# GpSimd waits for the spread of the scores of rounds 2 to 4

## The chip, the cores and the metric

The kernel runs on one core of one Trainium2 chip. The metric is the time of one execution on the device, in microseconds; several executions are taken and the median is given. The engines of the core are named as in the profile: PE is TensorE (matmuls), DVE is VectorE, ACT is ScalarE, POOL is GpSimd, SP is SyncE. They run side by side, each through its own list of instructions in order, and wait for each other by semaphores.

## The reference

The input `x` holds 128 sequences of 32 tokens with 128 features. A first block makes a gated recurrent layer with a normalization at its end, a second one a feed-forward layer for half of the tokens of each sequence.

```python
# first block (cut)
ctx = causal_ema(x, tau_ctx)
wg = sigmoid(einsum(concat[x, ctx], Wg) + bg);  gated = x * wg
mod = 0.5 + sigmoid(einsum(gelu(x @ Wn1.T + bn1), Wn2) + bn2)     # 128 time constants
traces = causal_ema(gated * mod, tau) for each of them
temporal = sum over them of traces * softmax(blend)
gate = sigmoid(temporal @ Wtemp.T + btemp);  soma = gelu(x @ Wsoma.T + bsoma)
out = (soma * gate) @ Wout.T
hidden = (out - mean) / sqrt(var + 1e-05) * gamma + beta
# second block (cut)
scores = einsum('bsd,d->bs', hidden, w_router)
top_scores, top_idx = top_k(scores, 16)                            # 16 of 32 tokens
h = gelu(selected @ W1 + b1);  processed = h @ W2 + b2
result = x + hidden, and at the selected tokens + sigmoid(top_scores) * processed
```

## The kernel before

The 4096 tokens are worked on in five rounds, of 1, 2, 2, 2 and 1 quads; a quad is 512 tokens, or four tiles of 128. The kernel is software-pipelined by hand: the string `ORDER` lists all steps as `kind:round.part`, and each engine walks through this one list and issues what it has to do of each step. So every engine executes its part in the order of `ORDER`, and steps of different rounds are interleaved in it. PE writes its results to a ring of eight PSUM banks, which other engines read.

The steps of a round, as far as they matter here:

- `unit` (16 for each round): PE multiplies (L1042), DVE multiplies the result by the gated input into one of three buffers `prod` (L817), POOL adds that to `ctx_acc` (L468). `sum` is POOL's last addition of a round (L476). `gate`: PE multiplies `ctx_acc` (L1049), ACT takes the tanh (L612). `soma_gate` is DVE's product of the two (L826, into `x_t`).
- `out`: PE (L1057), then ACT squares and copies to `o_sb` (L619, L631); `stats`: DVE adds the squares (L835); `var`: POOL adds the epsilon (L480) and takes the power -0.5 (L483).
- `score`: DVE multiplies the router's column of `o_sb` by that power, 8 numbers on each partition, 4 in rounds 0 and 4 (L842, into `small`), and lays the scores on a diagonal mask (L846, into `spread`), which raises `spread_done` by one.
- `bc`: PE multiplies `spread` by a matrix of ones within a sequence (L1061); DVE compares (L855, L856) and counts with `tie` (L863, L866). `pick`: DVE makes the selection matrix (L875, into `pick`) and weights it (L883, into `pick_w`, from `small` and `pick`).
- `normed`: ACT scales `o_sb` (L636, L639). `gather` (PE L1070, ACT L652, DVE L902), `up` (PE L1093 and L1098, ACT's gelu L673), `turn_pick` (PE L1081, ACT L663), `down` (PE L1109, DVE L907) and `scatter` (PE L1117, DVE L916 into `x_nat`) are the feed-forward layer. DMAs of SP then write `x_nat` out.
- `plus_beta` (POOL, L457: `x_nat` + beta) and `residual` (POOL, L491 and L496: `o_sb` times gamma, then added to `x_nat`) make the residual, which DVE's `scatter` of the same round needs.

In the late part of `ORDER` the steps around the three scores stand like this (steps of `unit` and `back` that stand between are cut where a line has "..."):

```
sum:3 unit:4.2 stats:2.1 var:2 carry:4.0 gather:1 unit:4.9 unit:4.8 gate:3 up:1.0 up:1.1 soma_gate:3
score:2 residual:1 scatter:0 normed:2 unit:4.5 out:3.0 unit:4.11 bc:2 tie:2 turn_pick:1 pick:2 down:1 ...
sum:4 stats:3.1 var:3 score:3 up:2.0 up:2.1 scatter:1 gate:4 bc:3 tie:3 soma_gate:4 normed:3 turn_pick:2
plus_beta:2 pick:3 down:2 plus_beta:3 residual:2 out:4.0 gather:3 stats:4.0 var:4 scatter:2 turn_pick:3
up:3.0 up:3.1 score:4 bc:4 normed:4 tie:4 pick:4 down:3 plus_beta:4 residual:3 gather:4 scatter:3 up:4.0 ...
```

POOL has nothing to do for `score`: it goes from `var:3` to `plus_beta:2`, for instance, as soon as PE has read `x_nat` for the last time.

Of the kernel before, what the change touches and what calls it, by code (L numbers as in the profile page):

```python
# [44 lines left out]
def tiles(r):  # L45
    return QUADS[r] * QT
# [138 lines left out]
def adaln_ffn(nc, x, tau_raws, w_n2, b_n2, blend, tau_ctx, w_g, b_g, w_n1, b_n1, w_soma, b_soma,  # L185
              w_temp, b_temp, w_out, gamma, beta, w_router, w_1, b_1, w_2, b_2, out):
    with ExitStack() as ctx:
# [204 lines left out]
        @block.gpsimd  # L392
        def _(pool):
            nc.gpsimd.memset(ident[:, :], 0.0).then_inc(own_pool, 1)
            pool.wait_ge(own_pool, 1)
            nc.gpsimd.affine_select(out=ident[:, :], in_=ident[:, :], compare_op=ALU.not_equal, fill=1.0,
                                    base=0, pattern=[[-1, P]], channel_multiplier=1).then_inc(ident_done, 1)
            nc.gpsimd.memset(ones[:, :], 1.0).then_inc(ident_done, 1)
            nc.gpsimd.memset(odd_even[:, :], 1.0).then_inc(own_pool, 1)
            nc.gpsimd.memset(eye_t[:, :], 0.0).then_inc(own_pool, 1)  # L400
            nc.gpsimd.memset(before[:, :], 1.0).then_inc(own_pool, 1)
            nc.gpsimd.memset(same_b[:, :, :], 1.0).then_inc(own_pool, 1)
            nc.gpsimd.memset(minus_half[:, :], -0.5).then_inc(own_pool, 1)
            nc.gpsimd.iota(rank_of[:, :], pattern=[[1, T], [0, BT]], base=0, channel_multiplier=0,
                           allow_small_or_imprecise_dtypes=True).then_inc(own_pool, 1)
            pool.wait_ge(own_pool, 7)
            for b in range(BT):
                rows = slice(b * T, (b + 1) * T)

                nc.gpsimd.affine_select(out=odd_even[rows, 0:1], in_=odd_even[rows, 0:1], compare_op=ALU.is_ge,  # L410
                                        fill=0.0, base=L - 1, pattern=[[0, 1]],
                                        channel_multiplier=-1).then_inc(masks_done, 1)
                nc.gpsimd.affine_select(out=odd_even[rows, 1:2], in_=odd_even[rows, 1:2], compare_op=ALU.is_ge,
                                        fill=0.0, base=-L, pattern=[[0, 1]],
                                        channel_multiplier=1).then_inc(masks_done, 1)
                nc.gpsimd.affine_select(out=eye_t[rows, :], in_=eye_t[rows, :], compare_op=ALU.not_equal, fill=1.0,
                                        base=0, pattern=[[-1, T]], channel_multiplier=1).then_inc(masks_done, 1)
                nc.gpsimd.affine_select(out=before[rows, :], in_=before[rows, :], compare_op=ALU.is_ge, fill=0.0,
                                        base=-1, pattern=[[-1, T]], channel_multiplier=1).then_inc(masks_done, 1)
            pool.wait_ge(masks_done, 4 * BT)  # L420
            places = rank_of[:, :].rearrange("p (j b) -> p b j", b=BT)
            for src, fill in ((places, -1.0), (same_b[:, :, :], 0.0)):
                nc.gpsimd.affine_select(out=src, in_=src, compare_op=ALU.is_ge, fill=fill, base=0,
                                        pattern=[[-T, BT], [0, T]], channel_multiplier=1).then_inc(own_pool, 1)
            pool.wait_ge(own_pool, 9)
            for src, fill in ((places, -1.0), (same_b[:, :, :], 0.0)):
                nc.gpsimd.affine_select(out=src, in_=src, compare_op=ALU.is_ge, fill=fill, base=T - 1,
                                        pattern=[[T, BT], [0, T]], channel_multiplier=-1).then_inc(masks_done, 1)
            owned = [9]

            def pool_owned():
                owned[0] += 1
                return owned[0]

            for step in STEPS:
                kind, r, k = step
                if kind == "table":
                    pool.wait_ge(powers_done, 1)
                    pool.wait_ge(turned_c, 1)
                    lags = slice(k * TG, (k + 1) * TG)  # L440
                    nc.gpsimd.tensor_tensor(decayed[:, lags, :], blend_w[:, None, :].to_broadcast([P, TG, E]),
                                            powers[:, lags, None].to_broadcast([P, TG, E]),
                                            ALU.mult).then_inc(full_tab, 1)
                elif kind == "powers":
                    pool.wait_ge(powers_done, 1)
                    for t in range(L):
                        last = nc.gpsimd.tensor_copy(falling[:, :, t:t + 1],
                                                     powers[:, None, L - 1 - t:L - t].to_broadcast([P, HT, 1]))
                    last.then_inc(falling_done, 1)
                elif kind == "plus_beta":  # L450
                    pool.wait_ge(full(("xt", r, 0)), filled(("xt", r, 0)))
                    if r not in SCANNED:
                        pool.wait_ge(full(("context", r, 0)), filled(("context", r, 0)))
                    if r == 0:
                        pool.wait_ge(rest_in, 2 * 16)
                    x_r = tiles_of(x_nat, r)
                    nc.gpsimd.tensor_tensor(x_r, x_r, beta_r[:, None, :].to_broadcast([P, tiles(r), E]),  # L457
                                            ALU.add).then_inc(xb_done, 1)
                elif kind == "unit" and k > 0:
                    n = PRODS.index(step)  # L460
                    dst = lagged(part(ctx_acc, r), r, k, shift=1)
                    pool.wait_ge(read(step), reads_after(step))
                    if add_before(step):
                        pool.wait_ge(acc_done, ADDED[add_before(step)])
                    else:
                        first = ("unit", r, 0)
                        pool.wait_ge(read(first), reads_after(first))
                    nc.gpsimd.tensor_tensor(dst, dst, packed(prod[:, n % NP, 0:width(r)], r, k),  # L468
                                            ALU.add).then_inc(acc_done, 1)
                elif kind == "sum":  # L470
                    for h in range(QUADS[r]):
                        back = ("back", r, h)
                        pool.wait_ge(read(back), reads_after(back))
                    pool.wait_ge(acc_done, ADDED[add_before(step)])
                    dst = part(ctx_acc, r)[:, L * batches(r):]
                    nc.gpsimd.tensor_tensor(dst, dst, carried[:, r % 2, 0:L * batches(r)],  # L476
                                            ALU.add).then_inc(acc_done, 1)
                elif kind == "var":
                    pool.wait_ge(stats_done, nth(last_of("stats", r)))
                    nc.gpsimd.tensor_scalar(small[:, r % 2, 4, 0:tiles(r)], small[:, r % 2, 5, 0:tiles(r)], 1e-5, None,  # L480
                                            ALU.add).then_inc(own_pool, 1)
                    pool.wait_ge(own_pool, pool_owned())
                    nc.gpsimd.tensor_tensor(small[:, r % 2, 7, 0:tiles(r)], small[:, r % 2, 4, 0:tiles(r)],  # L483
                                            minus_half[:, 0:tiles(r)], ALU.pow).then_inc(rstd_done, 1)
                elif kind == "residual":
                    pool.wait_ge(norm_done, BEFORE[r + 1] * QT)
                    if r:
                        pool.wait_ge(res_done, r)
                    else:
                        pool.wait_ge(scanned, len(SCANS))  # L490
                    nc.gpsimd.tensor_tensor(prod_res[:, 0:tiles(r), :], o_sb[:, r % 2, 0:tiles(r), 0:E],  # L491
                                            gamma_r[:, None, :].to_broadcast([P, tiles(r), E]),
                                            ALU.mult).then_inc(own_pool, 1)
                    pool.wait_ge(own_pool, pool_owned())
                    pool.wait_ge(xb_done, r + 1)
                    nc.gpsimd.tensor_tensor(tiles_of(x_nat, r), tiles_of(x_nat, r), prod_res[:, 0:tiles(r), :],  # L496
                                            ALU.add).then_inc(res_done, 1)
# [650 lines left out]
```

## Time and profile before

| | us |
|---|---|
| median of 3 runs | 192.11 |
| lowest and highest | 189.43, 192.43 |
| the profiled execution | 189.27 |
| its span, first to last instruction | 187.5 |

In the span PE is busy for 92%, DVE for 77%, POOL for 72% and ACT for 51%. The chain of work that ended last lies on PE for 76% of the span, on DVE for 11% and on POOL for 3%; among its lines on DVE are L842 and L846, with 3% of the span each. The table of costliest groups has POOL's L468 with 81.0 us in 75 instructions. The busy times are modelled for matmuls, so a PE that is 92% busy is not a PE at its peak. A share of the whole span says little about one stretch; the rows below are therefore taken from the timeline, where "[3.72 <-DVE spread L846]" behind an instruction means that its engine stood idle for 3.72 us before it, until DVE's L846 let it go.

### The profile page before, as it was taken

The page shows a single profiled execution, that of the slowest core. Times are in us where ns is not written, and L with a number is a line of the kernel's source. Part 1 is how long each engine was busy: PE and PEld are TensorE (multiplying, and loading weights), DVE is VectorE, ACT ScalarE, POOL GpSimd, SP SyncE. Part 2 cuts the span into 40 slices and gives each one's busy share as a digit, 9 for nine tenths or more (in the row PEclk, how much of TensorE's full clock was granted, in tenths as well). Part 3 has the DMA queues.
Part 4 walks back from the last instruction along what each step waited for, and adds up shares of the span by engine and source line. Part 5 has one row for each costly group of instructions (what it writes and reads, how often), then busy time and mean ns, then how long its engine had stood idle before and what let it go on. Part 6 is the DMA issues. An engine that isn't in the chain of part 4 may idle for free.

```text
span 187.5 us, 3480 instructions
## 1 busy us (share of the span) xinstructions
PE 172.6 (92%) x1154; PEld 130.4 (70%) x1154; DVE 143.6 (77%) x223; ACT 96.5 (51%) x177; POOL 134.8 (72%) x158
## 2 busy tenths in 40 slices
PE   5798999999999999999999999999999983994991
PEld 4485445877669588695769687688689943983881
DVE  1628897769997988859787887798789749858822
ACT  3548697264680141772505454578487465157030
POOL 7838000788897999979686988999797599529800
PEclk9999999999999999999999999999999997899999
DMA  5687000000000000000000000000002000303032
GB/s 128 167 209 201 0 3 0 0 2 5 0 0 0 3 0 3 0 0 0 3 2 0 0 3 2 0 0 3 2 0 59 0 2 0 112 3 112 0 112 59
DMA packets 12785, 5.62 MB, mean 30 GB/s; under 512 B 2880, under 2 KB 12640, under 8 KB 12768
## 3 DMA queue, kind: packets, MB, share of 16 engines
q1 hardware_dynamic: 11904, 5.20, 10.3%
q10 hardware_dynamic: 864, 0.20, 0.5%
q8 instruction: 10, 0.16, 0.4%
q14 instruction: 7, 0.06, 0.1%
HBM read 3.30 MB, written 2.10 MB: 29 GB/s over the span
## 4 chain that ended last, share of the span: by engine, by line
PE 76%; DVE 11%; issue 3%; POOL 3%; ACT 2%; DMA 2%; ACTq 0%; DVEq 0%; POOLq 0%
PE ring L1042 27%; PE ring L1109 6%; PE ring L1015 5%; PE ring L1026 4%; PE ring L999 4%; PE ring L978 4%; PE ring L1000 4%; PE ring L1049 4%; DVE small L842 3%; PE ring L1057 3%; DVE spread L846 3%; PE ring L1006 2%; PE ring L1032 2%; PE ring L992 2%; PE ring L966 2%
## 5 line engine op out<-in xcount | busy, mean ns | idle before, releaser
L468 POOL TENSOR_TENSOR ctx_acc<-ctx_acc,prod 128x256 f32<-128x256 f32 (+17 forms) x75 | 81.0, 1095 | 30.9 <-DVE prod L817 26.8
L817 DVE TENSOR_TENSOR prod<-ring,gm 128x256 f32<-128x256 f32 (+17 forms) x75 | 41.3, 577 | 8.9 <-PE ring L1042 7.4
L1042 PE MATMUL ring<-mod_hi,decayed_lo 128*128 128x512 f32 (+15 forms) x104 | 35.0, 374 | 0.0
L1042 PE MATMUL ring<-mod_lo,decayed_hi 128*128 128x512 f32 (+15 forms) x104 | 30.1, 326 | 0.0
L1042 PE MATMUL ring<-mod_hi,decayed_hi 128*128 128x512 f32 (+15 forms) x104 | 30.0, 327 | 0.0
L1042 PEld LDWEIGHTS ring<-mod_hi,decayed_lo 128*128 128x128 f32 x104 | 18.4, 189 | 7.6 <-issue 6.3
L1042 PEld LDWEIGHTS ring<-mod_lo,decayed_hi 128*128 128x128 f32 x104 | 19.2, 189 | 2.0 <-issue 1.2
L1042 PEld LDWEIGHTS ring<-mod_hi,decayed_hi 128*128 128x128 f32 x104 | 19.2, 189 | 0.9
L804 DVE TENSOR_TENSOR state<-ring,blend_w 128x1024 f32<-128x1024 f32 x16 | 18.8, 1219 | 1.1 <-PE ring L1015 0.9
L1109 PE MATMUL ring<-w_sb,gm 128*128 128x128 f32 x128 | 15.8, 282 | 0.1
L1109 PEld LDWEIGHTS ring<-w_sb,gm 128*128 128x128 f32 x128 | 15.4, 199 | 0.3 <-issue 0.3
L673 ACT ACTIVATE gm<-ring,b_c 128x512 f32<-128x512 f32 (+1 forms) x20 | 10.8, 599 | 4.8 <-PE ring L1098 4.5
L602 ACT ACTIVATE carried_nat<-ring 128x512 f32<-128x512 f32 x8 | 4.8, 598 | 15.2 <-PE ring L1026 15.2
L496 POOL TENSOR_TENSOR x_nat<-x_nat,prod_res 128x1024 f32<-128x1024 f32 (+1 forms) x5 | 10.0, 2008 | 0.4
L639 ACT ACTIVATE o_sb<-o_sb,small 128x128 f32<-128x128 f32 x32 | 9.8, 392 | 0.0
L457 POOL TENSOR_TENSOR x_nat<-x_nat,beta_r 128x1024 f32<-128x1024 f32 (+1 forms) x5 | 9.6, 1927 | 0.3 <-DMA gamma_r<-in_L_cond_gamma_dram 0.3
L612 ACT ACTIVATE ring<-ring,bias_h 128x1024 f32<-128x1024 f32 (+1 forms) x5 | 4.6, 918 | 9.6 <-PE ring L1049 9.6
L772 DVE TENSOR_TENSOR_SCAN ring<-prod_res,ring 128x1024 f32<-128x1024 f32 (+1 forms) x4 | 8.0, 2017 | 1.9 <-ACT x_t L532 1.7
L999 PE MATMUL ring<-x_t,turned_w 128*128 128x512 f32 x16 | 8.8, 634 | 0.5 <-ACT ctx_acc L532 0.5
L1061 PE MATMUL ring<-spread,same_b 128*128 128x256 f32 (+1 forms) x10 | 3.3, 412 | 6.5 <-DVE spread L846 6.5
L491 POOL TENSOR_TENSOR prod_res<-o_sb,gamma_r 128x1024 f32<-128x1024 f32 (+1 forms) x5 | 9.1, 1820 | 0.1
L1015 PE MATMUL ring<-gated_nat,mod_nat 32*128 32x256 f32 x128 | 9.2, 400 | 0.0
(168 smaller groups left out, 358.9 us busy)
## 6 DMA issues: line engine op xcount, KB each, us to landing
x_nat<-in_x_dram SPq DMA_DIRECT2D x3, 512.0 KB, 4.2
out_dram<-x_nat SPq DMA_DIRECT2D x3, 512.0 KB, 3.2
x_nat<-in_x_dram SPq DMA_DIRECT2D x2, 256.0 KB, 4.7
w_sb<-in_L_ffn_W_dram SPq DMA_DIRECT2D x2, 256.0 KB, 5.3
out_dram<-x_nat SPq DMA_DIRECT2D x2, 256.0 KB, 3.2
down<-in_cond_dram SPq DMA_DIRECT2D x2, 64.0 KB, 2.7
prod<-in_L_cond_Wg_dram ACTq DMA_DIRECT2D x1, 128.0 KB, 2.8
prod<-in_L_cond_Wsoma_dram ACTq DMA_DIRECT2D x1, 64.0 KB, 2.9
```

The source lines that it names most:

```text
L457: nc.gpsimd.tensor_tensor(x_r, x_r, beta_r[:, None, :].to_broadcast([P, tiles(r), E]), ALU.add).then_inc(xb_done, 1)
L468: nc.gpsimd.tensor_tensor(dst, dst, packed(prod[:, n % NP, 0:width(r)], r, k), ALU.add).then_inc(acc_done, 1)
L491: nc.gpsimd.tensor_tensor(prod_res[:, 0:tiles(r), :], o_sb[:, r % 2, 0:tiles(r), 0:E], gamma_r[:, None, :].to_broadcast([P, tiles(r), E]), ...
L496: nc.gpsimd.tensor_tensor(tiles_of(x_nat, r), tiles_of(x_nat, r), prod_res[:, 0:tiles(r), :], ALU.add).then_inc(res_done, 1)
L639: nc.scalar.activation(o_sb[:, r % 2, n, 0:E], o_sb[:, r % 2, n, 0:E], ACT.Copy, scale=small[:, r % 2, 7, n:n + 1]).then_inc(norm_done, 1)
L673: nc.scalar.activation(inner(r, f * n_sel, (f + 1) * n_sel), slot(step)[:, i * BANK:i * BANK + n_sel], ACT.Gelu_apprx_tanh, bias=b1_c[:, f ...
L804: nc.vector.tensor_tensor(state[:, q % 2, half, :], slot(step).rearrange("p (n e) -> p n e", e=E)[:, half, :], blend_w[:, None, :].to_broa ...
L817: nc.vector.tensor_tensor(dst, packed(slot(step), r, k), lagged(gated(r), r, k), ALU.mult).then_inc(read(step), 1)
L999: nc.tensor.matmul(dst[:, half], wgx_t, part(x_t, r)[:, half], start=True, stop=False)
L1015: last = nc.tensor.matmul(dst[:, at:at + 2 * E], mod_nat[rows, q % 2, i, :], gated_nat[rows, q % 2, i, :, :].rearrange("p o e -> p (o e)") ...
L1042: last = nc.tensor.matmul(to[:, c], w[:, k, :], src[:, c], start=(i == 0), stop=(i == len(parts) - 1))
L1109: last = nc.tensor.matmul(dst[:, n * E:(n + 1) * E], inner(r, at, at + P), w2_sb[:, f, :], start=first, stop=final)
```

## The change

In POOL's walk through `ORDER` a branch is added: at `score` of rounds 2, 3 and 4 POOL waits until DVE has written the spread of this round. POOL's next instruction is then L491 of `residual:1` in round 2, L457 of `plus_beta:2` in round 3 and L457 of `plus_beta:4` in round 4. No instruction is added, taken away or moved on any engine. Rounds 0 and 1 stay as they are.

```diff
@@ -482,6 +482,9 @@
                     pool.wait_ge(own_pool, pool_owned())
                     nc.gpsimd.tensor_tensor(small[:, r % 2, 7, 0:tiles(r)], small[:, r % 2, 4, 0:tiles(r)],
                                             minus_half[:, 0:tiles(r)], ALU.pow).then_inc(rstd_done, 1)
+                elif kind == "score" and r >= 2:
+
+                    pool.wait_ge(spread_done, r + 1)
                 elif kind == "residual":
                     pool.wait_ge(norm_done, BEFORE[r + 1] * QT)
                     if r:
```

## Rows read from the trace of the kernel before

**Rows 1.** The page, part 1: busy time, share of the span, instructions.

```profile
PE 172.6 (92%) x1154; PEld 130.4 (70%) x1154; DVE 143.6 (77%) x223; ACT 96.5 (51%) x177; POOL 134.8 (72%) x158
```

**Rows 2.** Timeline of DVE: start us, us, line, operation, count, idle before.

```profile
90.63 0.16 DVE L842 TENSOR_TENSOR small<-o_sb,small 128x4 f32<-128x4 f32 x1
90.83 0.29 DVE L846 TENSOR_TENSOR spread<-eye_t,small 128x128 f32<-128x128 f32 x1
...
137.99 1.89 DVE L842 TENSOR_TENSOR small<-o_sb,small 128x8 f32<-128x8 f32 x1
...
152.59 2.30 DVE L842 TENSOR_TENSOR small<-o_sb,small 128x8 f32<-128x8 f32 x1 [2.85 <-POOL small L483]
154.92 2.53 DVE L846 TENSOR_TENSOR spread<-eye_t,small 128x256 f32<-128x256 f32 x1
157.37 1.21 DVE L916 TENSOR_TENSOR x_nat<-ring,x_nat 128x1024 f32<-128x1024 f32 x1
158.82 0.43 DVE L855 TENSOR_TENSOR ring<-ring,small 128x256 f32<-128x256 f32 x1 [0.24 <-PE ring L1061]
...
162.78 0.69 DVE L883 SCALAR_TENSOR_TENSOR pick_w<-small,pick 128x512 f32<-128x512 f32 x1
...
169.03 1.25 DVE L842 TENSOR_TENSOR small<-o_sb,small 128x4 f32<-128x4 f32 x1 [0.34 <-POOL small L483]
170.32 2.23 DVE L846 TENSOR_TENSOR spread<-eye_t,small 128x128 f32<-128x128 f32 x1
173.19 0.30 DVE L855 TENSOR_TENSOR ring<-ring,small 128x128 f32<-128x128 f32 x1 [0.64 <-PE ring L1061]
...
175.34 1.09 DVE L883 SCALAR_TENSOR_TENSOR pick_w<-small,pick 128x256 f32<-128x256 f32 x1
176.76 0.69 DVE L907 TENSOR_TENSOR down<-ring,b_r 128x512 f32<-128x512 f32 x1 [0.33 <-PE ring L1109]
```

**Rows 3.** Timeline of POOL, same columns.

```profile
137.66 2.19 POOL L491 TENSOR_TENSOR prod_res<-o_sb,gamma_r 128x1024 f32<-128x1024 f32 x1
...
147.10 2.62 POOL L468 TENSOR_TENSOR ctx_acc<-ctx_acc,prod 128x192 f32<-128x192 f32 x4 [2.96 <-DVE prod L817]
...
150.88 1.67 POOL L483 TENSOR_TENSOR small<-small,minus_half 128x8 f32<-128x8 f32 x1
152.52 4.64 POOL L457 TENSOR_TENSOR x_nat<-x_nat,beta_r 128x1024 f32<-128x1024 f32 x2
157.12 2.37 POOL L491 TENSOR_TENSOR prod_res<-o_sb,gamma_r 128x1024 f32<-128x1024 f32 x1
...
167.65 0.23 POOL L480 TENSOR_SCALAR small<-small 128x4 f32<-128x4 f32 x1 [5.73 <-DVE small L835]
...
174.97 1.18 POOL L491 TENSOR_TENSOR prod_res<-o_sb,gamma_r 128x512 f32<-128x512 f32 x1
```

**Rows 4.** Timeline of PE, same columns.

```profile
141.59 3.74 PE L1109 MATMUL ring<-w_sb,gm 128*128 128x128 f32 x32
...
152.74 1.13 PE L1049 MATMUL ring<-ctx_acc,wtemp_t 128*128 128x512 f32 x2
157.59 1.19 PE L1061 MATMUL ring<-spread,same_b 128*128 128x256 f32 x2 [3.72 <-DVE spread L846]
...
159.43 4.30 PE L1109 MATMUL ring<-w_sb,gm 128*128 128x128 f32 x32
...
165.43 1.16 PE L1117 MATMUL ring<-down,pick_t 64*128 64x128 f32 x16
...
172.69 0.46 PE L1061 MATMUL ring<-spread,same_b 128*128 128x128 f32 x2 [2.75 <-DVE spread L846]
```

**Rows 5.** Windows of PE: stretch, us, busy, granted clock, DMA share, GB/s.

```profile
140.00:150.00 10.00, 10.00 (x84) 1.00 0.10 28
157.50:159.00 1.50, 1.41 (x4) 0.50 0.00 0
```

**Rows 6.** Timeline of ACT, same columns as rows 2.

```profile
168.61 2.63 ACT L673 ACTIVATE gm<-ring,b_c 128x512 f32<-128x512 f32 x4 [0.80 <-PE ring L1098]
```

## The prediction

> **What bounds the kernel now.** I read the page first: PE is busy for 92% of the span, POOL for 72%, DVE for 77% [rows 1]. A change to what POOL waits for can pay only where PE is not the limit, so I went down PE's own timeline and looked for its idle time. From 140 to 150 us it is busy throughout [rows 5]. Later it has two pauses: 3.72 us ahead of `bc:3` and 2.75 us ahead of `bc:4`, both ended by DVE's `spread` of L846 [rows 4]. `bc` stands ahead of the rest of PE's queue (`turn_pick`, `down`), so in both places everything waits for a score.
>
> The timeline of DVE says why the score is late [rows 2]. L842 multiplies 128x8 numbers. In round 0 its 128x4 form takes 0.16 us; in round 3 it takes 2.30 us, in round 4 1.25 us, in round 2 1.89 us. L846 takes 0.29 us in round 0 for 128x128, and 2.53 us (128x256) and 2.23 us (128x128) in rounds 3 and 4. The timeline of POOL [rows 3] shows what lies beside them: POOL ends its power (L483) at 152.55 and goes straight on to two L457 additions of 2.32 us each, from 152.52 to 157.16. L842 ends at 154.89, at the boundary between the two; L846 ends at 157.45, behind the second. So a DVE instruction of this kind that finds POOL busy stands until POOL's instruction ends. L883 in round 4 does so too: 1.09 us for 128x256, ending at 176.43, beside a POOL L491 from 174.97 to 176.15, though the 128x512 form in round 3 takes 0.69 us with POOL free. All three read both inputs from SBUF; L855 reads PSUM and SBUF and takes 0.43 us at 158.82, in the middle of a POOL multiplication [rows 2, 3].
>
> The Trainium skill, page "SBUF — State Buffer", the part on the engines' ports, says the same of a DVE instruction with two SBUF inputs against a GpSimd instruction that reads SBUF: exclusive, held for the whole instruction, and whichever starts first keeps it. It adds nothing to the sum, but by that rule a POOL that is made late can block a later DVE instruction as well as it blocked this one. The rows show this in L883 of round 4, and it is the main deduction below.
>
> **The change part by part.** It adds three waits, removes and moves nothing. Each holds POOL until the spread is written; what stands behind on POOL is `residual:1` in round 2, `plus_beta:2`, `plus_beta:3`, `residual:2`, `var:4` in round 3, `plus_beta:4`, `residual:3`, `residual:4` in round 4.
>
> Round 2. The two DVE instructions would run from 137.99 to about 138.6, where L842 alone lasted until 139.88; POOL, done with its additions at 137.66, resumes at 138.7, late by 1.0 us. It had 2.96 us of idle time at 147.10 [rows 3], so that is hidden; without that cover it costs 1.0 us. The gain of some 1.7 us on DVE meets a PE that has no gap here, so I take 0.1 us for it, with bounds of 0 and 0.3 (`down:1` on PE starts at 141.59 at any rate [rows 4]). I leave it out of the sum.
>
> Round 3. From the power's end at 152.55: L842 0.16 and L846 0.42 (twice the columns of the 0.29, 0.13 more) with 0.05 of dispatch each end at 153.2. POOL resumes at 153.3, 0.75 us late. PE is done with `gate:4` between 153.4 and 153.9 (1.13 us from 152.74 [rows 4]), so `bc:3` starts at 153.4 and not at 157.59. DVE's `scatter:1` (1.21 us) follows the spread and ends at 154.45; there L855 starts, which stood at 158.82: 4.4 us earlier. With the same steps between, L883 is ready at 162.78 - 4.4 = 158.4. POOL then is at: L457 153.3 to 155.6, L457 to 157.95, L491 (2.37) to 160.3. So L883 waits 1.9 us for L491 and ends at about 160.9. POOL's L496 (as many elements as L491, taken as 2.35) comes behind it and ends at 160.9 + 2.35 = 163.3.
>
> PE has meanwhile, at its full clock, done `bc`, `turn_pick` and `down:2` in 0.5 + 0.4 + 3.7 (the 3.74 at 141.59; at 159.43 it was 4.30), until 158.1, `out:4` and `gather:3` in about 0.9 each, until 159.9. It waits for DVE's `down:2`, which is behind L883: 160.9 + 0.69 = 161.6. So `scatter:2` starts at 161.6 and not at 165.43: 3.8 us earlier. The granted clock was 0.50 in 157.5 to 159.0, behind PE's long pause, that is 1.2 GHz [rows 5]; with the pause gone I expect 2.4 GHz there. That saves PE some 1.3 us, which is inside the wait for DVE and is no term.
>
> Round 4. DVE needs three instructions of 0.69 behind L883 up to `stats:4`: 162.9. POOL is free at 163.3; L480 and L483 took 1.35 us (167.65 to 169.00), so the power ends at 164.65 against 169.00. L842 and L846 end at 165.2. PE, from `scatter:2` at 161.6, has 4.5 us of work up to the end of `up:3` (165.43 to 169.94 before, where its idle 2.75 us began), so it is at `bc:4` at 166.1 against 172.69: 6.6 us earlier. `down:3` follows at 166.4; ACT's four activations of `up:3` (168.61, 2.63 us [rows 6]) move with `up:3` to 164.8 and end at 167.4, in time for its second half. It ends at 170.1.
> L883 is ready 2.15 us behind L855 (173.19 and 175.34), at 166.55 + 2.15 = 168.7. POOL: L457 165.25 to 166.5, L491 to 168.7, L496 2.35 more, to 171.1. This is a coin toss: L883 slips in between at 168.7 or waits until 171.1 and ends at 171.5. DVE's `down:3`, before at 176.76, then starts at 170.1 or at 171.5: 6.6 or 5.3 us earlier. What follows is a chain through DVE and PE with POOL soon done, and moves as a whole. **Sum: 5.3 to 6.6, I take 5.9 us.**
>
> The profiled execution took 189.27 us for a span of 187.5, so the sum gives 183.4. It lies by the lowest of the three runs (189.43); the other two are 2.7 and 3.0 higher and no row says why. From the median of 192.11 the sum is 186.2. Between the two I take 185.0.
>
> **The rivals.**
> (a) The stall moves to L883 nearly whole. For it speaks the 1.09 us at 175.34. POOL's next instruction could take hold ahead of DVE in round 3 too, so that L883 waits for L491 and L496, 2.35 us more. Then `scatter:2` is at 163.95, `bc:4` at 168.5, L883 of round 4 waits until 172.9, `down:3` starts at 173.3: a gain of 3.5 us, 185.8 from the profiled time and 188.6 from the median. Against it: L491 and L496 are parted by a wait of POOL for itself.
> (b) Nothing meets POOL later: L883 is free in both rounds. `scatter:2` starts at 159.9, PE reaches `bc:4` at 164.4, but POOL's power still ends at 164.0: a gain of 8.3 us, 181.0 or 183.8. Against it: POOL is busy without a pause from 153.3 to 162.7 by my times.
> (c) The wait does not bring it. If L842 and L846 were slow of themselves in the late rounds, the spread would come as late as before and POOL 4.9 us later: but POOL's `residual:2` has 5.73 us of idle behind it, so 0 to 1 us is lost, 189 to 193. The 0.16 and 0.29 of round 0 speak against it, and so do the ends that fall on POOL's ends.
> (d) Slower. In round 2 POOL waits for DVE, whose `score:2` stands behind `soma_gate:3`, which waits for ACT's tanh of `gate:3`. POOL's additions of round 4 (`unit:4.5` onward) lead to `sum:4`, `gate:4` and the third power, all on the path. It decides from a pause of 2.96 us on; by the rows it is 1.0. If the spread of round 2 came 6 us later than I have it, POOL would lose 4 us, offset by the gains of rounds 3 and 4 above. To end over 2% slower it would have to be 12 us later; or those gains fail as in (c), and the pause is 7 us: 195 to 196. Nothing in the rows points there.
>
> **How the numbers follow.** Forecast 0.60 (183.4 to 186.8 with the toss and the two bases), (a) 0.15, (b) 0.08, (c) 0.12, (d) 0.05. The range runs from 181.5, which keeps nearly all of (b), to 188.5, which keeps most of (a). Two per cent is 3.8 us (about what a measurement of this kernel can tell from no change). Forecast and (b) are faster by more, except where an unlucky spread between runs takes a part (0.03 of the forecast); a third of (a) is faster, the rest is within 2% with (c): faster 0.70, same 0.25, slower 0.05.
>
> **What would show it.** L842 and L846 in rounds 2 to 4 at 0.2 and 0.3 to 0.45 us each; POOL idle for about 1.0, 0.7 and 0.6 us, ended by `spread`; PE's gaps of 3.72 and 2.75 us ahead of `bc` gone, and the granted clock at its upper level near 158; L883 of round 3 at some 2.5 us, with a new gap of PE ahead of `scatter:2`. The forecast is wrong if L842 stays at 1 us or more, if L883 waits in neither round or for two of POOL's instructions, or if POOL's idle time at 147 is gone.

## The result and the profile after

| | before | changed |
|---|---|---|
| median, us (lowest to highest) | 191.91 (189.43 to 192.43) | 184.19 (184.11 to 185.21) |
| profiled execution, us | 189.27 | 184.11 |
| its span, us | 187.5 | 181.5 |

The changed kernel is faster: the ratio is 0.965, with a 95% interval of 0.955 to 0.975. Ratios, here and below, leave out executions over 1.5% above the fastest of the same kernel, while medians are taken over all, so the two differ a little (184.19 / 191.91 is 0.960). From here on line numbers of the changed kernel are three higher behind POOL's new branch: L845, L849 and L886 are the L842, L846 and L883 of before. The whole trace runs 0.5 us earlier than before already ahead of the first of the three waits (L845 of round 2 starts at 137.48, before at 137.99), so 5.5 of the 6.0 us of span belong to the change. The time of the profiled execution fell by only 5.2 us, because what lies outside the span grew from 1.8 to 2.6 us there; in the other three executions of the changed kernel it is 1.8 to 2.6.

The timeline of DVE in the changed kernel (start us, us, line, operation, count, idle before), beside [rows 2]:

```profile
137.48 0.16 DVE L845 TENSOR_TENSOR small<-o_sb,small 128x8 f32<-128x8 f32 x1
137.68 0.42 DVE L849 TENSOR_TENSOR spread<-eye_t,small 128x256 f32<-128x256 f32 x1
...
151.97 0.17 DVE L845 TENSOR_TENSOR small<-o_sb,small 128x8 f32<-128x8 f32 x1 [2.74 <-POOL small L483]
152.18 0.42 DVE L849 TENSOR_TENSOR spread<-eye_t,small 128x256 f32<-128x256 f32 x1
...
157.80 2.25 DVE L886 SCALAR_TENSOR_TENSOR pick_w<-small,pick 128x512 f32<-128x512 f32 x1
...
166.17 0.16 DVE L845 TENSOR_TENSOR small<-o_sb,small 128x4 f32<-128x4 f32 x1 [0.34 <-POOL small L483]
166.36 0.29 DVE L849 TENSOR_TENSOR spread<-eye_t,small 128x128 f32<-128x128 f32 x1
...
169.46 0.97 DVE L886 SCALAR_TENSOR_TENSOR pick_w<-small,pick 128x256 f32<-128x256 f32 x1
170.87 0.69 DVE L910 TENSOR_TENSOR down<-ring,b_r 128x512 f32<-128x512 f32 x1 [0.45 <-PE ring L1112]
```

The six instructions of the three scores take 0.16 to 0.42 us each; L842 and L846 had taken 2.30 and 2.53 us in round 3. L886 of round 3 takes 2.25 us, though; it had taken 0.69. `down:3` (L910) starts at 170.87 and not at 176.76.

The timeline of POOL in the changed kernel, beside [rows 3]:

```profile
138.18 2.20 POOL L494 TENSOR_TENSOR prod_res<-o_sb,gamma_r 128x1024 f32<-128x1024 f32 x1 [0.98 <-DVE spread L849]
...
146.49 2.61 POOL L468 TENSOR_TENSOR ctx_acc<-ctx_acc,prod 128x192 f32<-128x192 f32 x4 [2.12 <-DVE prod L820]
...
152.68 4.68 POOL L457 TENSOR_TENSOR x_nat<-x_nat,beta_r 128x1024 f32<-128x1024 f32 x2 [0.74 <-DVE spread L849]
157.31 2.19 POOL L494 TENSOR_TENSOR prod_res<-o_sb,gamma_r 128x1024 f32<-128x1024 f32 x1
159.58 2.67 POOL L499 TENSOR_TENSOR x_nat<-x_nat,prod_res 128x1024 f32<-128x1024 f32 x1
164.78 0.23 POOL L480 TENSOR_SCALAR small<-small 128x4 f32<-128x4 f32 x1 [2.53 <-DVE small L838]
...
166.73 1.27 POOL L457 TENSOR_TENSOR x_nat<-x_nat,beta_r 128x512 f32<-128x512 f32 x1 [0.60 <-DVE spread L849]
167.96 2.18 POOL L494 TENSOR_TENSOR prod_res<-o_sb,gamma_r 128x1024 f32<-128x1024 f32 x1
```

The three waits are the pauses of 0.98, 0.74 and 0.60 us ended by the spread, L849. The idle time ahead of the additions at 146.49 has shrunk from 2.96 to 2.12 us: the pause of round 2 was paid from it. L886 of round 3, which starts at 157.80, ends at 160.05, behind the L494 that ends at 159.50.

The timeline of PE in the changed kernel, same columns, beside [rows 4]:

```profile
153.21 0.59 PE L1064 MATMUL ring<-spread,same_b 128*128 128x256 f32 x2
...
154.08 3.74 PE L1112 MATMUL ring<-w_sb,gm 128*128 128x128 f32 x32
...
160.91 1.16 PE L1120 MATMUL ring<-down,pick_t 64*128 64x128 f32 x16 [1.32 <-DVE down L910]
...
163.52 0.47 PE L1096 MATMUL ring<-hid_hi,w_lo 128*128 128x512 f32 x1 [0.86 <-ACT hid_hi L655]
...
166.80 0.46 PE L1064 MATMUL ring<-spread,same_b 128*128 128x128 f32 x2 [0.28 <-DVE spread L849]
```

And that of ACT:

```profile
162.29 0.60 ACT L634 ACTIVATE o_sb<-ring 128x516 f32<-128x516 f32 x1 [2.94 <-POOL x_nat L499]
```

The pauses of 3.72 and 2.75 us ahead of `bc` are now nothing and 0.28 us. In their place stand 1.32 us ahead of `scatter:2`, which waits for DVE's `down:2` behind L886, and 0.86 us ahead of `up:3`, which waits for ACT's `hid_hi`. ACT's copy to `o_sb` (L634) stood for 2.94 us until POOL's L499 of `residual:2` was done: that wait is new.

The windows of PE in the changed kernel (stretch, us, busy, granted clock, DMA share, GB/s), beside [rows 5]:

```profile
156.00:160.00 4.00, 3.58 (x33) 1.00 0.15 41
```

The granted clock is 1.00, the level of 2.4 GHz, where it had been 0.50 between 157.5 and 159. `down:2` takes 3.74 us (L1112 at 154.08) and not 4.30.

### The profile page after: what moved, and what is told of

The parts are those of the page before. It is cut to its first block, busy times and chain, and to the rows that moved or that the text cites. A ratio compares the mean times of both kernels' runs of the same rounds, so it can differ in the third digit from the quotient of the medians.

```text
span 181.5 us, 3482 instructions
## 1 busy us (share of the span) xinstructions
PE 170.3 (94%) x1154; PEld 128.6 (71%) x1154; DVE 136.3 (75%) x223; ACT 96.3 (53%) x177; POOL 134.6 (74%) x158
## 4 chain that ended last, share of the span: by engine, by line
PE 76%; DVE 7%; POOL 7%; issue 4%; DMA 2%; ACT 1%; DVEq 0%; POOLq 0%; ACTq 0%
PE ring L1045 29%; PE ring L1018 5%; PE ring L1029 4%; PE ring L1112 4%; PE ring L981 4%; PE ring L1052 4%; PE ring L1060 3%; PE ring L1002 3%; DVE ring L775 2%; PE ring L1003 2%; PE ring L1096 2%; PE ring L1009 2%; DMA x_nat<-in_x_dram 2%; PE ring L1035 2%; PE ring L995 2%
## 5 line engine op out<-in xcount | busy, mean ns | idle before, releaser
L468 POOL TENSOR_TENSOR ctx_acc<-ctx_acc,prod 128x256 f32<-128x256 f32 (+17 forms) x75 | 81.0, 1098 | 29.8 <-DVE prod L820 25.7
L1112 PE MATMUL ring<-w_sb,gm 128*128 128x128 f32 x128 | 15.2, 276 | 0.1
L1112 PEld LDWEIGHTS ring<-w_sb,gm 128*128 128x128 f32 x128 | 14.7, 192 | 0.3 <-issue 0.3
L457 POOL TENSOR_TENSOR x_nat<-x_nat,beta_r 128x1024 f32<-128x1024 f32 (+1 forms) x5 | 9.6, 1927 | 1.3 <-DVE spread L849 1.3
L499 POOL TENSOR_TENSOR x_nat<-x_nat,prod_res 128x1024 f32<-128x1024 f32 (+1 forms) x5 | 10.1, 2016 | 0.4
L494 POOL TENSOR_TENSOR prod_res<-o_sb,gamma_r 128x1024 f32<-128x1024 f32 (+1 forms) x5 | 9.0, 1791 | 1.1 <-DVE spread L849 1.0
L1060 PE MATMUL ring<-wout_t,x_t 128*128 128x129 f32 x64 | 8.5, 276 | 0.0
```

The costliest lines, as they stand in the source:

```text
L1060: last = nc.tensor.matmul(dst[:, at:at + OW], part(x_t, r)[:, (k * QT + n) * P:(k * QT + n + 1) * P], wout_t[:, :], start=True, stop=True)
L1112: last = nc.tensor.matmul(dst[:, n * E:(n + 1) * E], inner(r, at, at + P), w2_sb[:, f, :], start=first, stop=final)
```

## The experiments

Ratios are against the kernel before, each with its 95% interval. The kernels were compared with before in several groups, so a difference between two of them is one between medians of different comparisons, good to some tenths of a microsecond.

| run | median, us | ratio |
|---|---|---|
| wait of round 2 alone | 191.36 | 1.004 (0.998 to 1.010) |
| wait of round 3 alone | 188.38 | 0.988 (0.979 to 0.996) |
| wait of round 4 alone | 186.93 | 0.981 (0.972 to 0.989) |
| changed kernel, `plus_beta:3` behind `residual:2` | 183.73 | 0.959 (0.953 to 0.965) |
| changed kernel, `plus_beta` early | 181.85 | 0.954 (0.944 to 0.964) |
| no waits, `plus_beta` early | 183.73 | 0.960 (0.953 to 0.966) |
| no waits, memset for `plus_beta:2` and `:3` | 188.46 | 0.983 (0.976 to 0.991) |
| changed kernel, also held until `pick_w` | 188.98 | 0.988 (0.981 to 0.995) |
| `plus_beta` early, waits, `residual:3` held | 181.08 | 0.948 (0.943 to 0.953) |

Where the interval reaches across 0.98 (the waits of round 3 and of round 4 alone, the memset), the kernel is faster, but whether by two per cent is not decided.

**The waits one by one.** The edit, for round 2 (3 and 4 likewise):

```diff
-                elif kind == "score" and r >= 2:
+                elif kind == "score" and r == 2:
```

> Only the wait of round 2 is kept. My theory (PE has no pause in round 2): the stall of L842 there goes (1.9 us to 0.2 us), POOL pauses for 1.0 us, its idle time ahead of the round 4 additions shrinks from 2.96 to about 2.1 us, and the time is that of before within 0.5 us. The stalls of rounds 3 and 4 stay: L842 and L846 together 4.8 and 3.5 us. Rival (every stall of DVE removed is time gained, or the change as a whole works through the earlier start): 1.7 us faster than before.

> Only the wait of round 3 is kept. My theory: bc of round 3 starts some 4 us earlier, then the chain waits for POOL's residual:2 as in the changed kernel, and round 4's stall of L842 and L846 (about 3 us) comes back: 2.5 to 3.5 us faster than before, about half of what the whole change gives. Rival (the stall of round 3 alone is the whole gain, round 4 would be hidden by PE's up step): 5.5 to 6 us faster.

> Only the wait of round 4 is kept. My theory: round 3 is as before (PE idle 3.7 us ahead of bc, the fall of the clock behind it), round 4's spread is 3 us earlier and bc follows up without a pause: 2.5 to 3 us faster than before. With the run of round 3 alone it adds up to the whole change. Rival (round 4 is hidden, or its gain is given back in the wait of L883 for POOL): 0 to 1 us faster.

The wait of round 2 alone gives nothing: 191.36 against 191.38 us. Its DVE row shows that it does its work all the same, as 1.90 us for L842 (round 2 of the run with the wait of round 3 alone) became 0.16:

```profile
137.73 0.16 DVE L845 TENSOR_TENSOR small<-o_sb,small 128x8 f32<-128x8 f32 x1
```

In these runs the stall is worth something only where PE would otherwise wait. The waits of rounds 3 and 4 alone give 3.0 and 4.5 us of the median. With 0.0 for round 2 that is 7.5, and the whole change gives 7.7. The executions of before fall on two levels, near 189.3 and near 192, and a difference of medians carries that mixture. Taken from the lowest execution to the lowest, the waits of rounds 3 and 4 alone give 1.4 and 2.9 us (189.08 to 187.69 and to 186.17), and the whole change 5.3 (189.43 to 184.11). So most of the whole is in the parts, exactly to no better than 1 us, and neither rival (round 3 alone brings it all; round 4 is hidden) holds. By the medians round 4 gave more than the 2.5 to 3 us expected; the clock, below, is why. In the run of round 3 alone, DVE's L845 and L849 of round 4 stood as before, and PE in front of them:

```profile
169.65 0.77 PE L1064 MATMUL ring<-spread,same_b 128*128 128x128 f32 x2 [3.27 <-DVE spread L849]
170.22 4.89 PE L1112 MATMUL ring<-w_sb,gm 128*128 128x128 f32 x32
```

**What the stall is.** In the kernel before, without waits, `plus_beta` of rounds 2 and 3 was replaced by a memset, which occupies POOL about as long but reads nothing. `prod` is dead by then. This kernel leaves beta out of the residual of rounds 2 and 3.

```diff
+                    if r in (2, 3):
+                        pool.wait_ge(acc_done, ADDED[("sum", 4, 0)])
+                        pool.wait_ge(xb_done, r)
+                        nc.gpsimd.memset(prod[:, :, :], 0.0).then_inc(xb_done, 1)
+                        continue
```

> The kernel before, without waits; plus_beta:2 and plus_beta:3 (additions that read SBUF) are replaced by POOL memsets of the dead prod buffers, 128x3072 each, estimated at 2.6 us each from the 128x128 memset of 0.20 us. So beta is left out of the residual in rounds 2 and 3. Theory (DVE stands because both engines read SBUF through the same interface): beside a memset, which reads nothing, L842 of round 3 takes 0.2 us and L846 0.4 us, and the time is 2.5 to 3.5 us below that of before, as with the wait of round 3 alone. Rival (a busy POOL blocks DVE whatever it does): L842 and L846 take 2 us or more each, time as before.

The timeline of POOL in this kernel:

```profile
152.36 5.47 POOL L459 MEMSET prod<- 128x3072 f32 x2
```

And that of DVE (L847 and L851 are the L842 and L846 of before):

```profile
152.44 0.17 DVE L847 TENSOR_TENSOR small<-o_sb,small 128x8 f32<-128x8 f32 x1 [2.88 <-POOL small L488]
152.65 0.42 DVE L851 TENSOR_TENSOR spread<-eye_t,small 128x256 f32<-128x256 f32 x1
...
166.64 1.22 DVE L847 TENSOR_TENSOR small<-o_sb,small 128x4 f32<-128x4 f32 x1 [0.35 <-POOL small L488]
167.89 2.23 DVE L851 TENSOR_TENSOR spread<-eye_t,small 128x128 f32<-128x128 f32 x1
```

POOL is busy from 152.36 on, two memsets of 2.7 us, and L847 takes 0.17 us beside it. In round 4, beside additions, both stall as before (1.22 and 2.23 us). So a busy POOL alone does not block DVE. The Trainium skill, "SBUF — State Buffer", section "Who interferes with whom", says that a DVE instruction with two SBUF inputs contends with a GpSimd instruction that reads SBUF, not with one that only writes it. The rows agree: 0.17 us beside a memset, 2.30 us beside an addition; and in the kernel before, L866, with one input in SBUF, took 0.70 us at 160.14, inside an L496 of POOL from 159.56 to 161.91. A memset differs from an addition in more than what it reads, and no run here takes that apart. The time, 188.46, is that of the wait of round 3 alone (188.38): taking the addition away and waiting it out are worth the same there.

**What is late now.** The changed kernel holds POOL's `residual:2` behind two additions of beta. ACT's copy to `o_sb` in round 4 waits for it, since rounds 2 and 4 share a half of `o_sb`. First only the order was changed:

```diff
-plus_beta:2 pick:3 down:2 plus_beta:3 residual:2
+plus_beta:2 pick:3 down:2 residual:2 plus_beta:3
```

> The changed kernel with plus_beta:3 moved behind residual:2; nothing else. My theory (ACT's copy L634 waits for residual:2): residual:2 ends 2.3 us earlier, at 159.8, L634's wait shrinks from 2.9 to about 0.5 us, bc of round 4 is about 1.0 us earlier; L883 of round 4 then waits longer for POOL, so 0.3 to 1.2 us faster than the changed kernel. Rival (L883 of round 3 is what delays, residual:2 is not): L883 waits as long as before, so no change.

The timeline of ACT in this kernel (L633 is the copy to `o_sb`):

```profile
160.13 0.60 ACT L633 ACTIVATE o_sb<-ring 128x516 f32<-128x516 f32 x1 [0.31 <-POOL x_nat L498]
```

That of DVE, in round 4:

```profile
168.44 2.48 DVE L885 SCALAR_TENSOR_TENSOR pick_w<-small,pick 128x256 f32<-128x256 f32 x1
```

And that of PE, at `bc:4`:

```profile
165.86 0.38 PE L1063 MATMUL ring<-spread,same_b 128*128 128x128 f32 x2
```

ACT's wait went from 2.94 to 0.31 us and `bc:4` is at 165.86. It was at 166.80 in the changed kernel, in a trace that ran 0.5 us earlier; so 1.4 us are won there. L885 (the L883 of before) of round 4 then gives most of it back: 2.48 us beside POOL, against 0.97. DVE's `down:3` starts at 170.85, 0.5 us earlier than in the changed kernel by the same count. The medians, 183.73 and 184.19, differ by 0.5 us. Their ranges (182.70 to 183.89, 184.11 to 185.21) do not overlap, but they come from different comparisons, so the gain in time is likely and small; the link from `residual:2` to ACT is what the rows show.

Then the opposite: POOL held longer, also until `pick_w` is written, so that L883 is free too.

```diff
+                elif kind == "pick" and r >= 3:
+                    pool.wait_ge(pick_done, r + 1)
```

> The changed kernel, and POOL also waits at pick of rounds 3 and 4 until DVE has written pick_w: behind plus_beta:2 in round 3, behind plus_beta of round 3 already done and ahead of plus_beta:4 in round 4. Theory (residual:2 is now the limit): L883 falls from 2.25 to 0.7 us in round 3 and to 0.5 us in round 4, but residual:2 ends at about 165.5 and not at 162.2, so ACT's copy L634 and everything behind it is 3 us later: 2 to 3.5 us slower than the changed kernel. Rival (L883's stall is the limit): 1 to 1.5 us faster than the changed kernel.

The timeline of DVE in this kernel, at `pick_w` of rounds 3 and 4:

```profile
158.41 0.69 DVE L888 SCALAR_TENSOR_TENSOR pick_w<-small,pick 128x512 f32<-128x512 f32 x1
...
174.43 0.43 DVE L888 SCALAR_TENSOR_TENSOR pick_w<-small,pick 128x256 f32<-128x256 f32 x1
```

That of ACT, at the copy to `o_sb`:

```profile
166.12 0.60 ACT L636 ACTIVATE o_sb<-ring 128x516 f32<-128x516 f32 x1 [6.17 <-POOL x_nat L501]
```

And that of PE, at `up:3`:

```profile
167.35 0.77 PE L1098 MATMUL ring<-hid_hi,w_lo 128*128 128x512 f32 x1 [5.48 <-ACT hid_hi L657]
```

L888 (the L883 of before) takes 0.69 and 0.43 us, no stall at all, and the kernel is 4.8 us slower than the changed one: ACT waits 6.17 us for `residual:2` and PE 5.48 us for ACT. That is more than the 2 to 3.5 us expected. This trace runs 0.6 us later than that of the changed kernel, so the copy itself is 3.2 us later (166.12 against 162.29), as foreseen; the rest is the granted clock, which fell behind PE's pause (0.76 from 169 to 173): PE needs 4.5 us from the start of `up:3` to `bc:4`, where it worked for 3.0 in the changed kernel. A wait costs what stands behind it.

**Beta out of the way.** `plus_beta` needs nothing but `x_nat`, which PE has read early on, and POOL is idle for 14.8 us ahead of its first L468 in the changed kernel. So:

```diff
-... plus_beta:0 wg:3 ...
+... plus_beta:0 plus_beta:1 plus_beta:2 plus_beta:3 wg:3 ...
-... unit:4.11 bc:2 ...
+... unit:4.11 plus_beta:4 bc:2 ...
```

> The changed kernel with all three waits, and plus_beta:1, 2 and 3 moved to directly behind plus_beta:0 (where POOL is idle for 14.8 us) and plus_beta:4 to behind unit:4.11 (idle 2.1 us). My theory of what is late now (residual:2 holds back ACT's copy L634, and L883 meets POOL in round 3): residual:2 runs right behind the spread of round 3 and ends at about 157.3, L883 of round 3 takes 0.7 us and not 2.25, L634's wait of 2.9 us goes, bc of round 4 starts about 2.9 us earlier, and L883 of round 4 waits for POOL by 1 to 2 us: 2.1 us faster than the changed kernel, about 182. Rival (the chain is set by PE and ACT there anyway): no change against the changed kernel. Rival (POOL's 9 us earlier delay the additions of rounds 1 and 2): slower by up to 2 us.

> The kernel before, without any of the waits, with the same plus_beta steps moved early as in e5_beta_early. My theory (a score stalls for whatever POOL instruction stands next, and only the wait helps): L842 and L846 of round 3 now wait for L491 and L496, 2.2 and 2.4 us; round 4 likewise, some 4 us together: within 1 us of the kernel before, thus 8 to 10 us slower than e5_beta_early. Rival (it was the amount of POOL work behind the score that delayed): as fast as e5_beta_early within 1 us.

In the kernel with the waits, the timeline of DVE at `pick_w` of rounds 3 and 4 (L885 is the L883 of before):

```profile
158.01 0.69 DVE L885 SCALAR_TENSOR_TENSOR pick_w<-small,pick 128x512 f32<-128x512 f32 x1
...
166.66 2.15 DVE L885 SCALAR_TENSOR_TENSOR pick_w<-small,pick 128x256 f32<-128x256 f32 x1
```

That of PE, at `bc:4`:

```profile
164.08 0.38 PE L1063 MATMUL ring<-spread,same_b 128*128 128x128 f32 x2
```

As expected: L885 of round 3 is free (0.69 us), `bc:4` starts at 164.08, which is 2.7 us before the 166.80 of the changed kernel (2.9 counted from `score:2`, which this trace has 0.2 us later), L885 of round 4 stands for 2.15 us, and the median is 2.3 us below that of the changed kernel (2.1 had been worked out).

Without the waits I had expected the time of before. It is 183.73 us, 8.0 us below it; that expectation was wrong. The timeline of DVE in this kernel (L841 and L845 are the L842 and L846 of before):

```profile
151.69 2.13 DVE L841 TENSOR_TENSOR small<-o_sb,small 128x8 f32<-128x8 f32 x1 [2.81 <-POOL small L482]
153.85 0.42 DVE L845 TENSOR_TENSOR spread<-eye_t,small 128x256 f32<-128x256 f32 x1
...
164.41 2.14 DVE L841 TENSOR_TENSOR small<-o_sb,small 128x4 f32<-128x4 f32 x1 [0.34 <-POOL small L482]
166.58 0.29 DVE L845 TENSOR_TENSOR spread<-eye_t,small 128x128 f32<-128x128 f32 x1
```

And that of POOL:

```profile
151.62 2.18 POOL L490 TENSOR_TENSOR prod_res<-o_sb,gamma_r 128x1024 f32<-128x1024 f32 x1
153.88 2.63 POOL L495 TENSOR_TENSOR x_nat<-x_nat,prod_res 128x1024 f32<-128x1024 f32 x1
```

L841 (the L842 of before) stalls for the whole multiplication L490, 2.1 us, as foreseen. L845 does not stall: 0.42 and 0.29 us. L495 must wait for L490's result, and in this gap L841 ends and L845 starts (153.85) ahead of L495 (153.88), which is then the one that stands (2.63 us). The two L457 of the kernel before depend on nothing of each other; the second had started (154.8) ahead of the end of L842 (154.89), and L846 stood for it as well. The trace of before had shown this already in round 2, where L842 stood for an L491 and L846 did not stand at all, while POOL's L496 started at 139.94:

```profile
139.92 0.42 DVE L846 TENSOR_TENSOR spread<-eye_t,small 128x256 f32<-128x256 f32 x1
```

The prediction used just this wait of POOL for itself as its argument against rival (a), and the expectation of this run forgot it. So about half of the stall hung on which two POOL instructions followed; that it is the dependence between them is read from the starts, since the kinds of instruction changed as well. PE's pauses ahead of `bc` are 1.41 and 1.71 us in this kernel, where before had 3.72 and 2.75, and the granted clock is 1.00 behind both. The rival, that the amount of POOL work is what counts, does not hold either: the waits still give 1.9 us on top (181.85 against 183.73).

Last, `residual:3` held back until `pick_w` of round 4 is written:

```diff
+                elif kind == "pick" and r == 4:
+                    pool.wait_ge(pick_done, r + 1)
```

> The kernel of e5_beta_early, and POOL also waits for pick_w of round 4 ahead of residual:3. L883 of round 4 then takes 0.43 us and not 2.15, DVE's down:3 starts when PE is done with it, 0.7 us earlier, and residual:3 comes some 3 us later, at 167.2 to 171.8, which delays DVE's scatter:3 but nothing on the path. My theory: 0.4 to 0.7 us faster than e5_beta_early, so 181.3. Rival (scatter:3 on DVE or its bank holds up PE's last steps, as in e8_until_pick): the same or up to 1 us slower.

The timeline of DVE in this kernel, at `pick_w` of round 4:

```profile
165.91 0.43 DVE L887 SCALAR_TENSOR_TENSOR pick_w<-small,pick 128x256 f32<-128x256 f32 x1
```

0.43 us for L887 (the L883 of before), and 181.08 us (180.75 to 181.55) against 181.85 (181.52 to 182.25). In the traces DVE's `down:3` starts at 167.40 against 168.73, but 0.75 of these 1.3 us were there already at `score:2`, so the hold itself brings 0.6. As the ranges touch, the gain is likely and not proved. The same kind of wait that cost 4.8 us in the run above costs nothing here: DVE's `scatter:3` does stand 2.54 us for `residual:3`, but in a stretch where DVE would otherwise have waited 2.73 us for PE's `down:4`. This is the lowest median that was found, 0.948 of before.

**The two levels of before.** The times of the kernel before fell near 189.3 and near 192. It was profiled twice more.

> The kernel before, unchanged, once more with a profile. Its times fall near 189.3 and near 192. Theory (it is TensorE's clock behind the pauses ahead of bc that makes the two levels): a profiled execution near 192 shows the granted clock at its lower level for longer than one near 189.3, 6 to 7 us behind the pause of round 3, or again behind that of round 4, with the same stalls of L842 and L846. Rival (DVE and POOL meet differently): other durations of L842, L846 or L883, same clock.

> The same as e10_before_again, a further execution with a profile, since a single one can fall on either level.

They took 191.97 and 191.77 us. The windows of PE in the profile of before (columns as above), and its `down:3`:

```profile
160.00:164.00 4.00, 4.00 (x35) 0.92 0.33 98
173.00:177.00 4.00, 4.00 (x38) 1.00 0.00 0
```

```profile
172.99 3.74 PE L1109 MATMUL ring<-w_sb,gm 128*128 128x128 f32 x32
```

The same windows in the first of the further profiles:

```profile
160.00:164.00 4.00, 4.00 (x24) 0.57 0.29 81
173.00:177.00 4.00, 3.10 (x14) 0.58 0.00 0
```

And its timeline of PE, in that further profile:

```profile
157.35 1.19 PE L1061 MATMUL ring<-spread,same_b 128*128 128x256 f32 x2 [3.70 <-DVE spread L846]
...
159.19 5.75 PE L1109 MATMUL ring<-w_sb,gm 128*128 128x128 f32 x32
...
173.90 0.77 PE L1061 MATMUL ring<-spread,same_b 128*128 128x128 f32 x2 [2.77 <-DVE spread L846]
174.46 4.99 PE L1109 MATMUL ring<-w_sb,gm 128*128 128x128 f32 x32
```

The pauses are those of before (3.70 and 2.77 us), and L842 and L846 of round 3 take 2.30 and 2.53 us as before. The granted clock is different: 0.57 in 160 to 164, where the first profile had 0.92, and 0.58 in 173 to 177, where it had 1.00. `down:2` and `down:3` (L1109) take 5.75 and 4.99 us, where they took 4.30 [rows 4] and 3.74 in the first profile. The two differences are 1.45 and 1.25, together 2.7 us, and 191.97 - 189.27 is 2.7. The second further profile has the same (0.61 and 0.57 in the same windows, 191.77 us). The Trainium skill, "TensorE: Matmul & The Clock Gate", the part on the clock gate, says that an idle TensorE is set back to the lower clock. The traces agree behind the pause of round 3 in all three profiles of before; behind that of round 4 the same 2.8 us are followed by the lower clock in the two further profiles and not in the first. What decides between the two was not found.

This is also why round 4 alone gave 4.5 us of the median and not 3, while it gave 2.9 from lowest to lowest. In that run `down:3` has no pause ahead of it and takes 3.81 us; in the run of round 3 alone it follows on a pause of 3.27 us and takes 4.89. The timeline of PE in the run of round 4 alone, at `down:3`:

```profile
171.01 3.81 PE L1112 MATMUL ring<-w_sb,gm 128*128 128x128 f32 x32
```

## Why the prediction was right

The median, 184.19 us, is 0.8 below the predicted 185.0 and inside the range. By its steps:

**The bound.** PE's two pauses, ended by the spread, were what there was to win. The run with the wait of round 2 alone, where PE has no pause, shows it from the other side.

**Round 2.** Predicted: POOL 1.0 us late, hidden, no gain. Measured: 0.98 us, idle time down to 2.12 us, and 191.36 against 191.38 us.

**Round 3.** Predicted: L842 and L846 at 0.16 and 0.42 us, L883 waiting for POOL's L491 until 160.9, `scatter:2` at 161.6. Measured: 0.17 and 0.42 us, L886 until 160.05, `scatter:2` at 160.91, with everything 0.5 us earlier from the start. The place where the stall went was foreseen, and its size (1.9 us predicted, 2.25 - 0.69 = 1.6 measured).

**Round 4.** Here a step was missing. I had `up:3` follow on `scatter:2` without a pause and POOL's own work set the time of the power. In fact POOL was idle for 2.53 us ahead of L480, and PE for 0.86 us ahead of `up:3`: both waited for ACT's copy, and this for `residual:2`. `bc:4` was at 166.80 where the prediction, less 0.5, gives 165.6. The reordering of `plus_beta:3` and the longer hold confirm this link in both directions. I named what stands behind POOL's wait and left out who waits for that outside DVE: the buffer that ACT writes. That the sum came out right all the same (`down:3` 5.9 us earlier, as said) is in part luck. Without the 0.5 us that were there before the change it is 5.4, near the lower end of 5.3 to 6.6, and it came by another way. The toss had DVE's `down:3` at 170.1, behind PE, or at 171.5, behind an L883 that stands for 2.4 us. In fact L886 stood for only 0.97 - 0.43 = 0.5 us and was done at 170.43, and DVE then waited 0.45 us more for PE (L910), which was 1.2 us late since `bc:4`. That lateness is nearly as large as the 1.4 us between the two sides of the toss.

**The step between profile and median.** The sum gave 183.4 from the profiled execution and 186.2 from the median, and I took 185.0 between them. The 2.8 us between the two were not a constant on top: they were PE at the lower clock behind the pauses that the change removes (1.45 and 1.25 us, as the further profiles showed). From the profiled execution, whose clock had come back sooner, the sum gave 183.4 against 184.11 us measured: 0.7 off. The span fell by 6.0 us, 0.5 of them ahead of the change, and the time outside the span, which was in no term, grew by 0.8. So 185.0 is close because it was put between two bases, not because a row gave it. From the median of before the change gained 7.7 us, of which 2.5 are more than the 5.2 us between the two profiled executions. I had row 5 with a clock of 0.50 behind the pause and called it "no term", since it is hidden behind DVE once L883 waits; I did not ask what it did in the executions that were not profiled.

**The range.** Two sums were slightly off, without weight for the verdict. The forecast was given as 183.4 to 186.8, but its own gain of up to 6.6 us from 189.27 reaches down to 182.7. Rival (b) has POOL's power end at 164.0, so the spread is done at about 164.6 and `bc:4` cannot start at 164.4: its gain is 8.1, not 8.3.

**The rivals.** (a), the stall moving whole to L883, would have shown POOL's L499 ahead of L886; L886 got in between. (b) is refuted by L886's 2.25 us. (c) by L845's 0.17 us, and (d) by the 2.12 us that were left in round 2.

## What to carry to other kernels

A wait added to an engine that is off the path can pay, if it keeps this engine's next instruction out of the way of a short one on the path; price it by the pause of the bounding engine behind the short instruction, not by the stall itself. Then follow what stands behind the added wait to everybody who waits for it, buffers to be overwritten included, and look first whether that work can be moved to where its engine is idle. Where runs of a kernel fall on two levels, look at the granted clock behind each pause before carrying the difference over to the changed kernel.

## What the runs showed of the hardware

- DVE instructions with both inputs in SBUF stood until POOL's addition or multiplication from SBUF ended, where that had started first (L842: 2.30 us for 0.17), and not for a POOL memset of 2.7 us (0.17 us).
- Two POOL instructions that follow at once can block two DVE instructions in a row (2.30 and 2.53 us); if the second must wait for the first one's result, DVE's second gets in ahead of it (2.13 and 0.42 us), and it is POOL's that is longer by some 0.3 us (L495 2.63, against 2.36 for the same addition in round 2 of the changed kernel).
- The same kernel with the same pauses of PE ran at the lower granted clock for longer in some executions (0.57 against 0.92 and 0.58 against 1.00 in the same windows), which is 2.7 us of 192; in the changed kernel, without these pauses, the times lie within 1.1 us, where those of before lay within 3.0 (four executions each).
